# Layer 2's routed tiles in portions of 3, 3 and 2 groups, earlier loads, and the next scores ahead of the values in every slot

## What is computed

```python
x = x + L0_xattn(layernorm(x), ctx); x = x + L0_ffn(layernorm(x))   # cosines; dense experts, gates by rank
x = x + L1_xattn(layernorm(x), ctx); x = x + L1_ffn(layernorm(x))   # one head; top 2 of 8 experts, F = 512
x = x + L2_xattn(layernorm(x), ctx); x = x + L2_ffn(layernorm(x))   # 16 heads
x = x + L3_xattn(layernorm(x), ctx); x = x + L3_ffn(layernorm(x))   # 16 heads; top 2 of 8, F = 256, biases
# L2_ffn: 0.5 * shared / 8 + 0.5 * routed, where
#   routed = sum over the top 2 of 8 experts of gate * ((silu(t @ w1) * (t @ w3)) @ w2), F = 512
#   shared = the same form for all rows with 8 x 64 hidden columns
```

## Time and profile before

| | us |
|---|---|
| median of 3 runs | 2083.99 |
| the profiled execution | 2078.15 |
| its span (first to last instruction) | 2075.3 |
| PE busy (products) | 1774.3, 85% |
| PEld busy (weight loads) | 1367.3, 66% |
| DVE busy | 1292.3, 62% |
| ACT busy | 930.4, 45% |
| POOL busy | 780.3, 38% |
| mean granted TensorE clock | 0.922 |

### The profile page before, as it was taken

The page is one execution under the profiler, slowest core; times in us unless marked ns, Lnnn a source line. Parts: engine busy times, 40 slices in busy tenths (PEclk is TensorE's granted clock), DMA queues, the critical chain, the costliest instruction groups (busy, mean ns, idle before and its releaser), DMA issues.

```text
span 2075.3 us, 35354 instructions
## 1 busy us (share of the span) xinstructions
PE 1774.3 (85%) x10807; PEld 1367.3 (66%) x10807; DVE 1292.3 (62%) x3531; ACT 930.4 (45%) x3214; POOL 780.3 (38%) x803
## 2 busy tenths in 40 slices
PE   2999999999999997988788899988899968787864
PEld 1677767777677797755566678766688845464663
DVE  2467777676777543456656767666666756666643
ACT  1222222232222232677665545566554557677622
POOL 2354546466465413212423220243221143343345
PEclk7899999899999999999888999989899979888977
DMA  6505014321420497532100739100548344351756
GB/s 152 217 5 207 21 63 139 108 105 37 113 75 28 143 332 259 165 116 68 29 21 15 255 117 326 49 25 19 206 130 300 101 130 120 105 137 53 202 178 202
DMA packets 168280, 263.23 MB, mean 127 GB/s; under 512 B 24028, under 2 KB 101534, under 8 KB 167838
## 3 DMA queue, kind: packets, MB, share of 16 engines
q1 hardware_dynamic: 145870, 231.26, 34.6%
q0 software_dynamic: 12288, 25.19, 4.1%
q10 hardware_dynamic: 9936, 4.53, 0.8%
HBM read 196.48 MB, written 82.46 MB: 134 GB/s over the span
## 4 chain that ended last, share of the span: by engine, by line
PE 39%; DVE 12%; ACT 10%; issue 5%; DMA 3%; SPq 2%; POOL 1%; ACTq 0%; DVEq 0%; POOLq 0%
PE Y L1063 7%; PE up L1045 7%; ACT prob L1232 5%; PE B L862 3%; PE up L978 3%; PE A L854 3%; PE up L1050 3%; PE D L872 2%; DMA wg<-list 2%; ACT probT L1238 2%; DVE nmax L1429 2%; ACT kbd L1220 2%; PE Y L987 1%; PE up L854 1%; PE Y L1015 1%
## 5 line engine op out<-in xcount | busy, mean ns | idle before, releaser
L1881 POOL DMA_INDIRECT list<-xn,pos x192 | 191.9, 1000 | 371.0 <-DVE pos L1578 194.6
L1951 POOL TENSOR_TENSOR hid<-tg,uc 128x512 f32<-128x512 f32 x168 | 217.8, 1297 | 230.4 <-DVE tg L1667 229.1
L1238 ACT ACTIVATE probT<-B 128x512 f32<-128x512 f32 x256 | 157.5, 615 | 252.9 <-PE B L862 252.5
L1286 ACT ACTIVATE tg<-up 128x512 f32<-128x512 f32 x168 | 100.3, 597 | 299.1 <-PE up L978 286.4
L987 PEld LDWEIGHTS Y<-wd,hid 128*128 128x128 f32 x1344 | 180.4, 196 | 72.9 <-issue 45.1
L1232 ACT ACTIVATE prob<-up,nmax 128x128 f32<-128x128 f32 x596 | 212.6, 391 | 3.7 <-DVE nmax L1429 3.7
L1664 DVE TENSOR_TENSOR uc<-up,ytmp 128x512 f32<-128x512 f32 x168 | 115.0, 685 | 147.1 <-PE up L978 130.3
L978 PE MATMUL up<-x2T,wg 128*128 128x512 f32 x336 | 199.8, 677 | 2.7 <-DVE tg L1667 2.7
L862 PEld LDWEIGHTS B<-const,prob 128*128 128x128 f32 x1024 | 125.6, 152 | 111.9 <-issue 105.3
L1771 DVE COPY xsT<-Y 128x128 f32<-128x128 f32 x255 | 73.4, 288 | 200.7 <-PE Y L1015 196.4
L862 PE MATMUL B<-const,prob 128*128 128x128 f32 x1024 | 174.8, 297 | 16.8 <-ACT probT L1238 16.2
(11 more groups left out here) (241 smaller groups left out, 3785.7 us busy)
## 6 DMA issues: line engine op xcount, KB each, us to landing
w_tile<-wt SPq DMA_DIRECT2D x43, 768.0 KB, 6.7
list<-w_tile SPq DMA_DIRECT2D x21, 1536.0 KB, 14.2
w_tile<-wt SPq DMA_DIRECT2D x45, 512.0 KB, 4.9
w_tile<-wt SPq DMA_DIRECT2D x55, 321.0 KB, 3.8
wg<-list SPq DMA_DIRECT2D x255, 64.0 KB, 3.8
wd<-wt SPq DMA_DIRECT2D x18, 768.0 KB, 6.1
list<-wu SPq DMA_DIRECT2D x186, 64.0 KB
wd<-wt SPq DMA_DIRECT2D x16, 512.0 KB, 5.0
```

Source lines behind the costliest of these rows:

```text
L1238: act.activation(probT[:, (2 * r + i) % 4, :, :], B4[:, :, :], ACT.Copy).then_inc(probT_done.sem, 1)
L1881: pool.indirect_dma_start(out=list_to(K, g)[:, :], in_=xn2[:, t, :], in_offset=None, out_offset=bass.IndirectOffsetOnAxis(ap=pos[:, g, s, ...
L1951: pool.tensor_tensor(hid[:, n % HRING, :], tg[:, n % 2, :], uc[:, n % 2, :], ALU.mult)\
```

## The change

- `ROUNDS`: layer 2's routed tiles in rounds of 3, 3 and 2 groups (31 + 31 + 23 tiles) instead of 4 and 4 (39 + 39). `SHARED`: three parts of 12, 8 and 12 tiles instead of two of 16. `SPAN` deals them over slots 24 to 95; layer 3's first two rounds stand in slots 97 to 107 and 108 to 119 instead of 89 to 103 and 105 to 119; the last three are where they were. `GATHERS` and `ADDS` for them follow.
- `awaits_round`: group 6 of layer 3 gathers in the ordinary places, since its round ended long before.
- `transfers`: at the end of each segment that is followed by a routed round (from layer 2's on), the next round's first four tiles are loaded ahead of the last three stores.
- `slot` of PE: `early` holds for every slot whose predecessor has attention too. Slots 88 to 95 leave `THREE`.
- The transposed norm of layers 0 and 2 is copied once, into x2T, where ACT wrote it twice (L1177, L1179); the router and the actor read it there.
- Trip -1: the products up of chunks 0 and 1 come right after the router's and the actor's products; the first four steps of group 1's layer 0 all stand at the trip's last step.

```diff
-ROUNDS = [(1, 0, 4), (1, 4, 4), (2, 0, 4), (2, 4, 4), (3, 0, 2), (3, 2, 2), (3, 4, 2), (3, 6, 1), (3, 7, 1)]
+ROUNDS = [(1, 0, 4), (1, 4, 4), (2, 0, 3), (2, 3, 3), (2, 6, 2), (3, 0, 2), (3, 2, 2), (3, 4, 2), (3, 6, 1), (3, 7, 1)]
...
-SHARED = [[(2, None, (g, t)) for g in range(g0, g0 + STEPS) for t in range(T)] for g0 in (0, 4)]
-SEGMENTS = [ROUTED[0], ROUTED[1], SHARED[0], ROUTED[2], SHARED[1], *ROUTED[3:]]
+SHARED = [[(2, None, (g, t)) for g in groups for t in range(T)] for groups in ((0, 1, 2), (3, 4), (5, 6, 7))]
+SEGMENTS = [ROUTED[0], ROUTED[1], SHARED[0], ROUTED[2], SHARED[1], ROUTED[3], SHARED[2], *ROUTED[4:]]
...
-SPAN = {1: (-9, 24), 2: (24, 42), 3: (42, 56), 4: (57, 74), 5: (74, 88), 6: (89, 104), 7: (105, 120), 8: (121, 132),
-        9: (132, 139), 10: (139, 142)}
+SPAN = {1: (-9, 24), 2: (24, 33), 3: (34, 52), 4: (52, 57), 5: (57, 75), 6: (75, 81), 7: (81, 96), 8: (97, 108),
+        9: (108, 120), 10: (121, 132), 11: (132, 139), 12: (139, 142)}
...
-THREE = list(range(0, SPAN[2][0])) + list(range(SPAN[5][1], PAIRS * len(CHAIN)))
+THREE = list(range(0, SPAN[2][0])) + list(range(SPAN[THIRD - 1][1], PAIRS * len(CHAIN)))
...
                if trip < 0:
+
+                    layer0 = [(0, s + LEAD)] + ([(1, s0) for s0 in range(LEAD)] if s == TRIP - 1 else [])
...
+            return first_of_round(K, g) and (K, g) != (3, 6)
...
-                    if rows is None and up_ is not None and TILES[up_][1] is not None:
-                        if up_ + 1 == LAST_ROUND:
-                            for n in range(LAST_ROUND, LAST_ROUND + 4):
+                    if rows is None and up_ is not None:
+
+                        stores = [n for n in range(up_ + 1 - BEHIND, up_ + 1)
+                                  if TILES[up_][1] is not None and not stored_by_act(n)]
+                        for n in stores[:-DEPTH]:
+                            store_tile(n)
+                        if up_ + 1 < len(TILES) and TILES[up_ + 1][1] is not None and up_ + 1 >= FIRST[2]:
+                            for n in range(up_ + 1, up_ + 5):
                                 load_tile(n)
                                 load_weights(n)
-                        for n in range(up_ + 1 - BEHIND, up_ + 1):
-                            if not stored_by_act(n):
-                                store_tile(n)
+                        for n in stores[-DEPTH:]:
+                            store_tile(n)
...
-                early = lambda S: S in THREE and S - 1 in THREE
+                early = lambda S: around(S)[0] and around(S - 1)[0]
...
+                    if g < 0 and s + LEAD == 15:
+                        pe.wait_ge(rest_loaded, REST)
+                        up_product(0)
+                        up_product(1)
...
-                rows, out_ = (A, D, X, X)[K], (xnT2 if w == LN2 else xnT)[:, :] if K else xnT0
+                rows, out_ = (A, D, X, X)[K], normed(K, g, w)
                 act.activation(out_, rows[:, :], ACT.Copy).then_inc(xnT_done[K > 0][w].sem, 1)
-                if w == LN2 and K in (0, 2):
-                    act.activation(x2T[:, g % 2 if K == 0 else g % 4, :], rows[:, :], ACT.Copy).then_inc(x2T_done.sem, 1)
```

More of the change, by code:

```diff
@@ L75 @@
 STEPS = GROUPS // 2
-ROUNDS = [(1, 0, 4), (1, 4, 4), (2, 0, 4), (2, 4, 4), (3, 0, 2), (3, 2, 2), (3, 4, 2), (3, 6, 1), (3, 7, 1)]
-LIST_OF = [0, 1, 2, 0, 1, 2, 0, 1, 2]
+ROUNDS = [(1, 0, 4), (1, 4, 4), (2, 0, 3), (2, 3, 3), (2, 6, 2), (3, 0, 2), (3, 2, 2), (3, 4, 2), (3, 6, 1), (3, 7, 1)]
+LIST_OF = [u % 3 for u in range(len(ROUNDS))]
 MAX_TILES = 40
@@ L351, in scores_in, with normed @@
                 return [A4, F4, U4][Q % 3]
-            return [U4, A4, F4][(Q - 2 * SPAN[5][1]) % 3]
+            return [U4, A4, F4][(Q - 2 * SPAN[THIRD - 1][1]) % 3]
+        def normed(K, g, w):
+            if w == 1 and K in (0, 2):
+                return x2T[:, g % 2 if K == 0 else g % 4, :]
+            return (xnT2 if w else xnT)[:, :] if K else xnT0
         YT = Y[:, 0:P]
@@ L512, in stored_by_act @@
         def stored_by_act(n):
-            return n < FIRST[1] or n >= FIRST[9]
+            return n < FIRST[1] or n >= FIRST[ALONE]
         def list_of(u):
@@ L912, in actor_hidden @@
             def actor_hidden(g):
-                pe.wait_ge(x2T_done.sem, x2T_done.at(0, g, 1))
-                pe.matmul(A[0:ACTOR, :], aw1[:, :], xnT0, start=True, stop=True).then_inc(act1_psum.sem, 1)
+                pe.wait_ge(xnT_done[0][LN2].sem, xnT_done[0][LN2].at(0, g, 1))
+                pe.matmul(A[0:ACTOR, :], aw1[:, :], normed(0, g, LN2), start=True, stop=True).then_inc(act1_psum.sem, 1)
             def actor_logits(g):
@@ L993, in trip @@
                 for s, chunk, groups0, group1, s1, turns in in_trip(g):
-                    if chunk is not None:
+                    if chunk is not None and chunk >= 2:
                         up_product(chunk)
@@ L1115, in slot @@
                         pe.wait_ge(xnT_done[1][LN2].sem, xnT_done[1][LN2].at(*behind, 1))
-                        if behind[0] == 2:
-                            pe.wait_ge(x2T_done.sem, x2T_done.at(*behind, 1))
                     elif now:
@@ L1793, in slot @@
                     divide_heads(*before_last, rb // 2)
-                if r == 1 and ahead and not first_of_round(*ahead):
+                if r == 1 and ahead and not awaits_round(*ahead):
                     combine(*ahead, 0)
                 if r == 2 and ahead:
-                    if first_of_round(*ahead):
+                    if awaits_round(*ahead):
                         for s in range(2):
@@ L1872, in scatter @@
                     u = round_of(K, g)
-                    if u == 6:
-                        for s in range(2):
-                            pool.wait_ge(gathered[s].sem, gathered[s].at(3, GROUPS - 1, 16 * T))
-                    if u > 6 and g == ROUNDS[u][1]:
-                        pool.wait_ge(added, 2 * last_group(u - 3) + 2)
+                    if u > 2 and g == ROUNDS[u][1]:
+                        before_L, last = ROUNDS[u - 3][0], last_group(u - 3)
+                        if before_L == 3:
+                            pool.wait_ge(added, 2 * last + 2)
+                        else:
+                            for s in range(2):
+                                pool.wait_ge(gathered[s].sem, gathered[s].at(before_L + 1, last, 16 * T))
                 pool.sem_inc(alone, 1)
```

40 lines of the change are left out of this document (20 added, 20 removed).

## The result

| | before | after |
|---|---|---|
| median, beside each other | 2084.27 us | 2019.55 us |
| ratio, 95% interval | | 0.9684 [0.9654, 0.9714] |
| the profiled execution, its span | 2078.15, 2075.3 | 2020.92, 2018.8 |
| mean granted TensorE clock | 0.922 | 0.950 |
| PE busy | 1774.3, 85% | 1760.4, 87% |

A forecast was written before the change was run, and what follows sets the result against it. One-tile slots were taken as bound by a chain from last exponential through copy, values, scores and transposition, three-tile slots as PE 93% busy. Terms -60 + 0 - 4 - 4 = -68 gave 2010, set at 2013 us, range 1975 to 2052.

The forecast's parts named there:

- Portions: Slots 24 to 95: layer 2's rounds of 3, 3 and 2 groups take 664 us; -60 us, bounds -23 and -89.
- The line between the regimes: Upper price for slots 24 to 95: 8.4 us a slot, 2.13 us per tile above the first, 701 us.
- the packed slot: Slots 24 to 95 if PE alone sets the slot: 635 us.
- The lower price: Slots 24 to 95: 4.27 us a slot without a tile plus 2.8 us per tile, 635 us.
- Rival 1: Slots 24 to 95: the chain stays the bound, tiles cost by the line, 701 us; median 2050; 18%.
- Rival 2: PE packs fully, waits and low clock vanish: 635 us for the 72 slots, 1978 in all; 13%.
- Rival 3: Slots 34 to 95: PE's work alone counts, moving tiles wins nothing, seven more cost 19.6 us; +12, 2093; 6%.
- rival 4: Early scores stall PE at the second exponential in 64 slots: +64 us on top of Rival 1, 2110; 3%.
- The early scores: Next scores ahead of the values in all slots: at most 1.1 us per slot, 15 us, not added to the sum.
- Slots 96 to 120: Sooner loads save 6 us at slot 105 against twelve more layer 3 tiles: 0, bounds -6 and +10.
- The start: First products up moved behind the router, third chunk's product at 63 to 64: -4 us, bounds +1 and -6.
- From slot 121 on: Loads issued some 7 us sooner at slot 132, PE free at about 1991.6: -4 us, bounds -1 and -6.

The follow-up runs named there:

- the second profile: The changed kernel run and profiled again with nothing altered: 2029.78 us, ratio 0.9727 to the kernel before.
- the uneven deal: The changed kernel with the same tiles in slots 24 to 74, routed nearly three a slot, shared under one: 2068.36 us, ratio 0.9929 to the kernel before.
- the two runs: Early scores taken out of the changed kernel except where three banks are free (2043.69 us, 0.9804); early scores alone put into the kernel before (2062.75 us, 0.9919).

## Why the prediction was right, and where it wasn't

**The sum.** It had -60 + 0 - 4 - 4. Measured in the profiles: -55.4 in slots 24 to 95, -0.4 in slots 96 to 120, +1.4 at the start of slot 0 (with slots 0 to 23: -0.2), -0.5 from slot 121 on. The forecast stood on one term, and that was off by 8% (12% by the second profile's 671.3 us).

**Portions.** The line between the regimes gave 701 us, the packed slot 635, and I took 664; measured 668.4. The two bounds were less sound than that hit. Both took the regimes as one and three tiles a slot, where 16 tiles in 18 slots are 0.89 and 39 in 14 are 2.79. With these the line's slope is 4.27 / 1.90 = 2.25 us per tile, and it gives 72 x 8.39 + 53 x 2.25 = 723 us for the new stage: no gain instead of 23 us. The lower price becomes 12.66 - 2.79 x 2.8 = 4.86 us a slot and 677 for the stage, which was undercut; only from PE's busy time in the dense stages ((163.9 + 165.7) / 28 = 11.77 us a slot) does a floor follow: 3.97 us a slot without a tile and 613 us for the stage. The 9.3 us taken for most slots lay between two wrong prices, drawn to the one measured two-tile slot; that it hit is in part luck. By stage, forecast and measured: slots 24 to 33 83 and 86.0; 34 to 51 9.3 and 9.31 us a slot; 52 to 56 48 and 49.2; 57 to 74 9.3 and 9.67; 75 to 80 60 and 59.4; 81 to 95 138 and 132.2. The reason given (PE's own work fills such a slot) is what the plain slots show, PE busy 100% of 8.8 us. What I did not see is that two kinds of time remained: the first slot of a group (12 us), whose wait for the context load was already in the kernel before as slots 48 and 80, and the exponentials' wait. Without the first, slots 34 to 51 take 160.8 us, 8.9 each.

**Rivals.** Rival 1, the line, would have been 33 us more (55 with its slope put right): the uneven deal shows that its premise is false, since the same tiles cost 34 to 39 us more when they pile up. Rival 2 (635 us) lies 33 below; with the context load moved the stage stands at 657.1, with 46.7 us of idle time left, so PE doesn't pack fully. Rival 3 (PE's work alone counts, +12) falls by the result itself: 96.6 us of idle time was real and 39.8 of it could be had. In rival 4 PE's queue waits for the second exponential in 64 slots; the wait exists, but in 14 slots and for 19.3 us in total (18.6 and one of 0.7 by the other bank), just under the 20 set as the point where I would have been wrong. That point was badly chosen: with the context load moved the waits total 21.0 us (20.3 and 0.7) and the kernel is faster, and taking the early scores away costs 9 to 12 us more than it gives back in these slots. In uneven slots that wait doubles (38.6 us in 29 waits). The 2110 us given for rival 4 should read 2114 by its own terms (2078.15 - 31 + 64 + 3).

**The early scores** were my reason to stand under the line, at up to 15 us; the two runs measure 9 to 12 us and 22 us. Here the size was right and the account incomplete: in the kernel before the gain shows as PE's busy time, at a higher clock, and hardly as idle time.

**Slots 96 to 120.** 0 was forecast and -0.4 came (+2.3 in the second profile). The working holds in its parts: the boundaries at a round's first rows cost 6 to 9 us without the early loads, and the denser slots 97 to 119 take 7.5 us each, as the 7.2 to 7.4 of the earlier trace rows said.

**The start** is the step that failed: -4 forecast, and slot 0 began 1.4 us later. Two things. First, the chain was already 3.3 us late at the first transposition of the second norm (44.92 against 41.60), ahead of every instruction that the change moves. 1.6 us of it were there already at the scaling of the first norm (21.43 against 19.87); 1.6 more was one group of sixteen products of the key's norm (L807), which took 3.54 us instead of 1.91, in most kernels with the new code and in one of them not. Both parts are no effect of the change: the kernel before with only its context load moved has them too (scaling at 21.35, 3.54 us, transposition at 44.84). Their cause stays open. Second, of the own gain of 4 only 2.4 to 3 came. The products up moved forward as said (50.40, 3.7 us after the router's product), but I had followed PE and DVE and not ACT's queue. In order of time, ACT, then DVE, end of trip -1:

```profile
65.31 0.60 ACT L1196 ACTIVATE w_tile<-A 128x512 f32<-128x512 f32 x1 [3.92 <-PE A L775]
65.81 0.59 ACT L1303 ACTIVATE tg<-up 128x512 f32<-128x512 f32 x1
...
66.43 0.69 DVE L1684 SCALAR_TENSOR_TENSOR tg<-tg,up 128x512 f32<-128x512 f32 x1 [1.72 <-ACT tg L1303]
67.03 0.68 DVE L1681 TENSOR_TENSOR uc<-up,ytmp 128x512 f32<-128x512 f32 x1
69.75 0.69 DVE L1684 SCALAR_TENSOR_TENSOR tg<-tg,up 128x512 f32<-128x512 f32 x1 [2.04 <-ACT tg L1303]
```

Chunk 0's tanh (L1303) stands behind ACT's copy of group 1's transposed norm (L1196), and the change moved that norm behind the gates. ACT was idle 3.92 us and the chunk's product long done. That is the +1 side of my bounds (the transposition comes later), which I had costed for PE and not for ACT's order.

**From slot 121 on,** -4 was forecast, -0.5 came. From slot 127 on it is -2.6: SP, then PE, which answers to the earlier trace rows:

```profile
1915.70 13.45 SPq L708 DMA_DIRECT2D list<-wu  x9
1929.97 0.35 SPq L690 DMA_DIRECT2D wg<-list  x1
...
1935.48 1.12 PE L775 MATMUL up<-const,xn 128*128 128x128 f32 x4 [1.41 <-DVE xn L1415]
...
1938.32 1.71 PE L910 MATMUL up<-wr,xnT 128*128 128x8 f32 x8
```

Nine stores stand ahead of the first load instead of twelve, PE is at no row's wait, and the router's product follows its norm's transposition by 2.8 us. The whole end is less certain than that: with the new code and its early loads it took 108.4 to 111.0 us over the profiles, with the old code 111.0 to 114.0. The 2.5 us that slot 121 lost to the gathers between the scatters I had passed over: POOL is a queue too, and `GATHERS` moved on it.

**The rule weighed.** The Trainium skill, "Perfetto Trace Analysis", section Identifying the Most-Contended Engine, wants the weight loads' share in place of the products' busy time. The trace agrees in part: the dense stages had 80% of it, and over the 72 slots it went from 493.69 / 723.8 = 68% to 489.79 / 668.4 = 73%, so there was room. But where PE is busy all through a slot the share is already 80 to 90% (6.88 / 8.60 in slot 48 with the context load moved, 7.92 / 8.80 in slot 49 of the changed kernel), and whether the rest can be had no run tests. The prediction set the same page's Optimization Strategy against this change, and rival 3 under its name. That reading was too narrow: the section asks to find the gaps on that engine and to end what they wait for, and says that interleaving regimes may pay. Here PE got 175 instructions more, its idle time in the 72 slots fell by 39.8 us, and the kernel became 3.2% faster: the trace agrees with the section, and not with rival 3.

## What to carry to other kernels

When a stage with idle time and a stage that is full alternate, deal the work evenly even at the price of more of it: with the same tiles the even deal took 34 to 39 us less than the uneven one, and the whole stage gained 55 us although the smaller rounds that made it possible added 20 us of products. Before trusting a slot price, list the slots that don't follow it: the first slots of the groups stood in the old profile at 14.1 and 18.3 us, and one load moved within one in-order queue was worth another 12 to 17 us. Where a step moves, follow every engine's queue past it, those of ACT and POOL too.

## What was not expected of the hardware

- A slot with 0.7 tiles takes as long (8.2 to 8.6 us) as one with 1.2 (8.6): PE rests, and its granted clock in such a stage is 0.84 to 0.87 against 0.92, so that its products take longer. Work put into the gaps came at a higher clock: PE's busy time in slots 24 to 95 fell by 15.6 us while its instructions grew.
- The context load's move changed the median by 17.5 us, clear of the spread of its four runs (2005.01 to 2018.99, against 2028.39 to 2034.91), while edits worth 2 to 3 us could not be told from the clock's own spread: slot 0 began anywhere from 849.7 to 861.3 us in kernels whose first 850 us are nearly the same.
- Sixteen products of one column (L807) took 1.91 or 3.54 us at the same place in programs that differ elsewhere, old code and new. No experiment here says why.
